# The loops of the message layer written out, and three staging copies taken out, in a graph network on one core

## The reference

```python
node_feat = mlp(x, W_node, ...)                       # relu(x W + b), then normalised over all rows
edge_feat = mlp(edge_attr, W_edge, ...)               # 4 features per edge become 96
message = concatenate([x[row], x[col], edge_feat])    # row: source of the edge, col: its target
message = mlp(message, W_msg, ...)                    # relu, then normalised over all edges
agg = segment_sum(message, col)
out = layernorm(x + agg + node_feat)
```

## Time and profile before

| | us |
|---|---|
| median of 3 runs (5089.65 to 5105.41) | 5099.98 |
| the profiled execution | 5108.32 |
| its span in the trace | 5106.6 |

### The profile page before, as it was taken

How to read it: one execution, slowest core, us unless ns; L and a number is a source line. 1 busy time by engine, 2 the same in 40 slices (tenths; PEclk the granted TensorE clock), 3 DMA queues, 4 the chain that set the end, 5 groups by cost and what they waited for, 6 DMA issues and landing times. The chain is left out here.

```text
span 5106.6 us, 84268 instructions
## 1 busy us (share of the span) xinstructions
PE 4049.7 (79%) x30821; PEld 3591.3 (70%) x30821; DVE 1971.3 (39%) x5418; ACT 1413.1 (28%) x2193; POOL 1885.2 (37%) x1813
## 2 busy tenths in 40 slices
PE   5888889989997999899965444444457888888886
PEld 1232289989996999899965444444457888788776
DVE  8989911121114111311143222222255444444444
ACT  5757800000001000000013222222244444444444
POOL 1001100010002100200027777777707777777772
PEclk9999999989997999999976666565567777777875
DMA  4434566646664666566631111111121111111111
GB/s 170 188 160 183 226 257 251 245 173 221 250 246 152 234 239 237 198 237 237 238 133 38 40 39 39 39 39 39 39 69 41 40 40 41 41 41 41 42 41 32
DMA packets 182512, 670.85 MB, mean 131 GB/s; under 512 B 88343, under 2 KB 109591, under 8 KB 137111
## 3 DMA queue, kind: packets, MB, share of 16 engines
q1 hardware_dynamic: 128024, 584.38, 31.5%
q0 software_dynamic: 54272, 83.47, 7.7%
HBM read 532.11 MB, written 135.60 MB: 131 GB/s over the span
## 5 line engine op out<-in xcount | busy, mean ns | idle before, releaser
L947 PE MATMUL ps<-arena 128*120 128x288 bf16 x13720 | 1750.3, 288 | 63.2 <-POOL arena L568 47.7
L947 PEld LDWEIGHTS ps<-arena 128*120 128x120 bf16 x13720 | 1690.2, 134 | 77.3 <-POOL arena L568 53.8
L1611 POOL DMA_INDIRECT arena<-table,idx_st x832 | 918.2, 1104 | 395.1 <-issue 265.2
L1115 POOL DMA_INDIRECT arena<-table,idx_st x832 | 790.6, 950 | 276.3 <-issue 254.1
L742 DVE TENSOR_REDUCE spare<-ps 120x96 f32<-120x288 f32 x280 | 128.1, 458 | 1428.2 <-PE ps L947 1428.2
L1820 PE MATMUL ps<-M,arena 96*128 96x96 f32 x1664 | 479.6, 389 | 177.4 <-DVE arena L1741 173.9
L1345 PE MATMUL ps<-arena 128*96 128x128 f32 x1664 | 367.2, 412 | 226.4 <-DMA arena<-table,idx_st 226.4
L903 PE MATMUL ps<-arena,spare 128*128 128x500 bf16 x1664 | 449.3, 382 | 81.5 <-DVE spare L713 50.0
L1345 PEld LDWEIGHTS ps<-arena 128*96 128x96 f32 x1664 | 343.1, 274 | 239.7 <-issue 238.1
L1820 PEld LDWEIGHTS ps<-M,arena 96*128 96x128 f32 x1664 | 361.9, 269 | 183.7 <-issue 183.4
L620 ACT ACTIVATE arena<-ps 128x1000 bf16<-128x1000 f32 x416 | 415.5, 1004 | 164.1 <-PE ps L903 137.2
(11 more groups left out here) (314 smaller groups left out, 4477.3 us busy)
## 6 DMA issues: line engine op xcount, KB each, us to landing
arena<-blocks_dram SPq DMA_DIRECT2D x280, 1500.0 KB, 6.3
blocks_dram<-arena SPq DMA_DIRECT2D x70, 1500.0 KB, 5.0
arena<-table,idx_st POOLq DMA_INDIRECT x1664
table<-TAB SPq DMA_DIRECT2D x28, 336.0 KB, 3.2
arena<-qtable SPq DMA_DIRECT2D x104, 72.0 KB
table<-X SPq DMA_DIRECT2D x21, 336.0 KB, 2.6
ea_dram<-arena SPq DMA_DIRECT2D x1, 4992.0 KB, 13.6
arena<-ea_dram SPq DMA_DIRECT2D x1, 4992.0 KB
```

The costliest lines, as they stand in the source:

```text
L947: last = nc.tensor.matmul(apply_ps[m % 2][0:w, :], blk[m % 3][:, b, 0:w], Hs[:, b, :], start=b == 0, stop=b == NB - 1)
L1115: eng.indirect_dma_start(out=rows[r % 2][:, u, :], out_offset=None, in_=table[:, :], in_offset=bass.IndirectOffsetOnAxis(ap=idx_st[r][:, u ...
L1611: eng.indirect_dma_start(out=rows[r][:, u, :], out_offset=None, in_=table[:, :], in_offset=bass.IndirectOffsetOnAxis(ap=idx_st[r][:, u:u + ...
```

## The change

GpSimd, SyncE, ScalarE, VectorE and TensorE have the message layer's loops over groups written out: all 104 groups stand one after another with fixed addresses. The copies of lines 1646, 1728 and 1729 are taken out. GpSimd reads the indices in `idx_all` and waits on `q["hs"]` itself; its first two groups wait only for the 2 that VectorE adds at the start of the layer. TensorE reads the edge features in `ea6` and the valid column in `w_all`, and no longer waits for the copy. The order of all other steps on each engine stays.

```diff
             @block.gpsimd
-                    with eng.Fori(0, NG // 2) as i:
-                        for r in range(2):
-                            eng.wait_ge(idx_staged, (k + K * PH) * NG + i * 2 + r + 1)
-                            eng.sem_inc(pool_gate, 1)
-                            for u in range(U):
-                                eng.indirect_dma_start(
-                                    out=rows[r][:, u, :], out_offset=None, in_=table[:, :],
-                                    in_offset=bass.IndirectOffsetOnAxis(ap=idx_st[r][:, u:u + 1], axis=0)).then_inc(gathered[r], 16)
+                    for g in range(NG):
+                        eng.wait_ge(q["hs"], k * NG + max(g + 1, 2))
+                        eng.sem_inc(pool_gate, 1)
+                        for u in range(U):
+                            eng.indirect_dma_start(
+                                out=rows[g % 2][:, u, :], out_offset=None, in_=table[:, :],
+                                in_offset=bass.IndirectOffsetOnAxis(ap=idx_all[:, g, u:u + 1], axis=0)).then_inc(gathered[g % 2], 16)
             @block.sync
-                    with eng.Fori(0, NG // 2) as i:
-                        for r in range(2):
-                            g = i * 2 + r
-                            at = eng.value_load(basek_i[0:1, bass.ds(g, 1)], min_val=0, max_val=NP)
-                            eng.wait_ge(q["pre"], k * NG + g + 1)
-                            eng.dma_start(qwin[r][:, :], qtable[bass.ds(at, P), :]).then_inc(q_win[r], 16)
+                    for g in range(NG):
+                        at = eng.value_load(basek_i[0:1, g:g + 1], min_val=0, max_val=NP)
+                        eng.wait_ge(q["pre"], k * NG + g + 1)
+                        eng.dma_start(qwin[g % 2][:, :], qtable[bass.ds(at, P), :]).then_inc(q_win[g % 2], 16)
             @block.scalar
-                    def stage(g, r):
-                        wait("hs", g - 2)
-                        eng.sem_inc(act_gate, 1)
-                        nc.scalar.activation(idx_st[r][:, :], idx_all[:, bass.ds(g, 1), :].rearrange("p a u -> p (a u)"),
-                                             ACT.Copy).then_inc(idx_staged, 1)
...
+                    for g in range(NG):
+                        messages(g, g % 2)
+                        if g + 2 < NG:
+                            operands(g + 2, g % 2)
+                            features(g + 2, g % 2)
             @block.vector
-                eng.sem_inc(q["ea"], 2)
...
                         one_hot(eng, ohb[s], g, iotak).then_inc(q["oh"], 1)
-                        nc.vector.tensor_scalar(valid[s][:, :], w_all[:, bass.ds(g, 1), :].rearrange("p a u -> p (a u)"), 1.0, None, ALU.mult)
-                        nc.vector.tensor_scalar(ea_st[r][:, :], ea6[:, bass.ds(g, 1), :].rearrange("p a c -> p (a c)"),
-                                                1.0, None, ALU.mult).then_inc(q["ea"], 1)
...
+                    for g in range(NG):
+                        step(g)
             @block.tensor
-                        wait("ea", g)
                         wait("eaTs", g - 1)
-                        nc.tensor.transpose(ea_ps[:, 0, :], ea_st[r][:, 0:KE], identb[:, :])
-                        nc.tensor.transpose(ea_ps[:, 1, :], ea_st[r][:, KE:2 * KE], identb[:, :]).then_inc(q["eaT"], 1)
+                        nc.tensor.transpose(ea_ps[:, 0, :], ea6[:, g, 0:KE], identb[:, :])
+                        nc.tensor.transpose(ea_ps[:, 1, :], ea6[:, g, KE:2 * KE], identb[:, :]).then_inc(q["eaT"], 1)
...
-                            last = nc.tensor.matmul(ps[0:F, P:P + 1], sqbuf[r][:, u, :], valid[s][:, u:u + 1],
+                            last = nc.tensor.matmul(ps[0:F, P:P + 1], sqbuf[r][:, u, :], w_all[:, g, u:u + 1],
                                                     start=(u == 0), stop=(u == U - 1))
...
+                    for g in range(NG):
+                        step(g)
```

More of the change, by code:

```diff
@@ L104, in build @@
         small = sb("small", [P, 64])
-        valid = [sb(f"valid{i}", [P, U]) for i in range(4)]
         work_all = sb("work_all", [P, 4 * CB * P])
@@ L1585, in build @@
         v_link, sp_gate = sem("v_link"), sem("sp_gate")
-        names = "oh ea eaT eaTs ohT ohTs er ers pre hs relu hi sq rem mid lo msq".split()
+        names = "oh eaT eaTs ohT ohTs er ers pre hs relu hi sq rem mid lo msq".split()
         q = {name: sem(f"q_{name}") for name in names}
@@ L1669, in messages @@
                         nc.scalar.activation(hp[r][1], hrest, ACT.Copy).then_inc(q["mid"], 1)
[L1671 to L1681, removed]
                     for g in range(2):
@@ L1693, in _ @@
                 K = passes(eng)
-                eng.sem_inc(q["ea"], 2)
                 for name in names:
-                    if name != "ea":
-                        eng.sem_inc(q[name], 2)
+                    eng.sem_inc(q[name], 2)
                 link = Chain(eng, k_link, K * (PH * 4) + PH * 4, 4)
@@ L1723, in hots @@
                     def hots(g, s, free=False):
-                        r = s % 2
                         if not free:
@@ L1759, in low, with step @@
                         nc.vector.tensor_tensor(hp[r][2], hrest, hp[r][1], ALU.subtract).then_inc(q["lo"], 1)
[L1761 to L1765, removed]
+                    def step(g):
+                        r = g % 2
+                        add_rows(g, r, g // 2)
+                        if g + 2 < NG:
+                            hots(g + 2, (g + 2) % 4, free=g < 2)
                         rest(g, r)
-                        if not (first and d == 0):
+                        if g:
                             accumulate_sums(g - 1, 1 - r)
                         low(g, r)
-                        if ahead == 2:
+                        if g + 2 < NG:
                             transposed(g + 2, r)
@@ L1837, in sums, with step @@
                         for u in range(U):
-                            last = nc.tensor.matmul(ps[0:F, P:P + 1], sqbuf[r][:, u, :], valid[s][:, u:u + 1],
+                            last = nc.tensor.matmul(ps[0:F, P:P + 1], sqbuf[r][:, u, :], w_all[:, g, u:u + 1],
                                                     start=(u == 0), stop=(u == U - 1))
                         last.then_inc(summed, 1)
[L1842 to L1848, removed]
+                    def step(g):
+                        if g + 1 < NG:
+                            preact(g + 1, (g + 1) % 2, (g + 1) // 2)
+                        if g + 2 < NG:
+                            operands(g + 2, (g + 2) % 4)
+                        sums(g, g % 4)
                     operands(0, 0)
```

## The result

The changed kernel takes 5148.75 us, the median of 4 runs (5146.15 to 5151.89), against 5099.85 us before (also 4 runs): a ratio of 1.0098, with a 95% interval from 1.0081 to 1.0116. The change makes the kernel 0.98% slower. The forecast was 5145 us.

What follows compares the result with a forecast made beforehand. POOL's unbroken issue of gathers was taken as the bound. First to last add goes from 1171.2 to 1216.8 us, less 0.6 at the start: 45 us more, 5153 profiled, 5145 us forecast, range 5120 to 5178.

Steps and rivals of the forecast that it cites:

- The bound: Message layer: POOL issues gathers without a pause, and the layer ends one step after its last gather is issued.
- The index copy: ScalarE's copy gone: line 1755 starts 0.35 us earlier, holds the third gather, and steps take 11.8 us (11.7 to 12.05).
- the step of group 102: Step in the kernel before without index copy, with fixed addresses; taken as the model for every step, line 1755 at 2.82.
- the sum: First to last add: 28 + 100 x 11.8 + 7 x 1.25 = 1216.8 us, against 1171.2 before.
- The start: First 16 gathers can run some 15 us earlier; first three steps take 28 us (25 to 29), 28.7 before.
- The two VectorE copies: Lines 1728 and 1729 gone: nothing in the steps, 0.6 us off the first add (0 to 1).
- The written-out loops: Loop turns save nothing; POOL's seven longer gaps stay at 1.25 us each; code fetches taken as zero, at most 12 us.
- The first (the copies hold the gather): VectorE's copies, not the one-hot, hold the second gather: steps of 10.55 us, 5020 us, faster; chance 0.05.
- the second (the tie settles the other way): Line 1755 comes no earlier or the third gather goes first in all steps: about 11.0 us, 5065 us; chance 0.05.
- the third (the mixture stays): The mixture of steps stays as it is, or another phase gives the same mean: 5100 us; chance 0.04.
- the fourth: Dearer than forecast: steps of 12.05 to 12.1 us (5172), or fetches that hold POOL (5157); chance 0.08.
- The tie: Kernel before: line 1755 starts at 3.17, the third gather at 3.21; the gather won there, line 1755 in 28 steps.

Runs made afterwards that it cites:

- Experiment 2: The kernel before with only ScalarE's index copy taken out and POOL's loop written out; other loops and both VectorE copies stay: 5161.50 us, ratio 1.0122.
- experiment 5: The changed kernel with the two VectorE copies (valid column, edge features) put back and TensorE reading them: 5148.93 us, ratio 1.0099 to the kernel before.
- experiment 3: The changed kernel with an unread 128x480 copy added on ScalarE ahead of the relu: 5071.75 us, ratio 0.9949 to the kernel before.
- experiment 6: The changed kernel with the one-hot made by eight tensor_scalar instructions in place of one tensor_tensor: 5043.09 us, ratio 0.9895 to the kernel before.
- experiment 7: The changed kernel with VectorE's one-hot moved behind the remainder subtraction and the additions: 5092.38 us, ratio 0.9992 to the kernel before.

## Why the prediction was right

**The bound.** POOL's issue of gathers set the end before and after; the add waits for a gather in 101 steps.

**The index copy.** This was the step that carried the loss, and it came as worked out from the step of group 102: line 1728 at 2.82, the third gather 1.39, the fourth 1.56, steps of 11.84 in the median against 11.8 in the forecast. The first to the last add took 1217.1 us; the sum had 1216.8. Experiment 2 shows that this part alone gives the loss.

**The start.** The first three steps take 28.0 us, as taken. POOL does begin with the first gather at 3819.3 in place of 3838.1, waits 13.55 us ahead of its 17th, and gains nothing by it. The first add came 2.4 earlier instead of 0.6, which is within what it varies by.

**The two VectorE copies.** Priced at nothing: experiment 5 gives 0.2 us.

**The written-out loops.** 76 more fetches (227 against 151) cost nothing that shows: POOL has the same seven gaps of 2.0 to 2.2 us as before. What the loops' turns had cost was hidden as well, except on ScalarE, where the turn delays the relu (experiment 2); that small gain, 7 us, I had not priced.

**The number.** Profiled execution against profiled execution the forecast was 5153 and the measurement 5150.69. The terms behind it fit to within 2 us each, and the gain of 1.0 behind the last add was in no term. That the sum came so near is in part luck, since the first add alone moves by up to 9 us between kernels. The ends of the range do not come out of its terms: -10, -3 and -8 give 5124, and +25, +12 and +8 give 5190, where 5120 and 5178 stand. By either the measured time lies inside.

**The rivals.** The first (the copies hold the gather) falls with the timeline after, where the second gather is held by the one-hot with no copy behind it, and with experiment 5; the second (the tie settles the other way) also with the timeline, the third (the mixture stays) with the time, the fourth with the mean step. The tie itself was real: experiment 3 brings it back, 0.14 us later, and the gather wins.

## What to carry to other kernels

Where GpSimd issues indirect DMAs without a pause, look at how long each takes beside the VectorE instructions that run at its start; long ones with two SBUF inputs stretch it, and in a periodic loop the phase fixes which gathers are hit. Taking work off an engine that is not the bound moves that phase, and can cost more than the work: shift such an instruction so that no read falls under it, or split it into short instructions with a single SBUF tensor each, even if they take longer together, as in experiment 6. A step written out at the end of a loop is a free preview of the loop written out.

## What the runs showed of the hardware

- A gather that reads during a tensor_tensor on two SBUF inputs ends 0.81 to 0.83 us after the end of that instruction, or of the one that follows it at once, in all kernels on the two usual chips; alone it takes 0.94 to 0.96. The add of 1714 (79 gathers in the changed kernel) and the copy of 1708 (28), which read PSUM, held none.
- Other VectorE instructions on SBUF differ: a tensor_scalar of 0.65 us held the one gather that read under it, under the eight short tensor_scalar none of 126 gathers lost over 0.13 us (experiment 6), and a tensor_reduce of 6.66 us held none of six.
- Two such instructions in immediate succession hold one gather together (1.89 us, experiment 7), while a small tensor_scalar that follows the one-hot at once doesn't add to the hold (experiment 5). The reverse order, short tensor_scalar and then a tensor_tensor, can hold a gather through both (up to 2.76 us, on the third chip). What decides this was not tested.
- Two chips agree on the kernel before within 0.1% (5098.29 and 5096.06), and a third takes 5668.85 for it.
